# A gated attention and expert kernel: one stage order across the ends of token quarters, operand sums into buffers of their own, router inside the opening stage

## The reference, cut to what matters

```python
x = x + tanh(g_xattn[0]) * attention(layernorm(x), ctx_1024, Wq, Wk, Wv, Wo, bo)   # causal, 16 heads
x = x + tanh(g_ffn[0]) * ffn(layernorm(x))                                          # 4096 tokens x 512
...
scores = jax.nn.softmax(x @ router_w, axis=-1)             # 8 experts
topk_w, topk_idx = jax.lax.top_k(scores, 6)
g = jnp.einsum('td,edf->etf', x, w_gate)                   # 512 -> 256 each
u = jnp.einsum('td,edf->etf', x, w_up)
f_all = jnp.einsum('etf,efd->ted', jax.nn.silu(g) * u, w_down)
y = sum of the 6 picked f_all, each times its weight
y = y + _glu_mlp(hidden_states, ws_gate, ws_up, ws_down)   # shared, 512 -> 512
```

## Time and profile before

| | us |
|---|---|
| median of 3 runs | 1986.26 |
| lowest, highest | 1985.63, 1987.22 |
| profiled execution: span | 1984.3 |
| PE busy in it | 1888.9 |
| DVE busy | 1548.0 |
| ACT busy | 959.9 |
| POOL busy | 676.5 |

### The profile page before, as it was taken

The page is one execution under the profiler, slowest core; times in us unless marked ns, Lnnn a source line. Parts: engine busy times, 40 slices in busy tenths (PEclk is TensorE's granted clock), DMA queues, the critical chain, the costliest instruction groups (busy, mean ns, idle before and its releaser), DMA issues.

```text
span 1984.3 us, 33284 instructions
## 1 busy us (share of the span) xinstructions
PE 1888.9 (95%) x11664; PEld 1599.0 (81%) x11664; DVE 1548.0 (78%) x3333; ACT 959.9 (48%) x2252; POOL 676.5 (34%) x851
## 2 busy tenths in 40 slices
PE   6999999999998489999999999998999999899999
PEld 6899999999997368888867888876888887788887
DVE  5889888888888677787887777787777787777776
ACT  4777777777777343333433333343333343333332
POOL 3122132122221544343443334443334344433431
PEclk8999999999999689999999999999999999999999
DMA  7565565565554211212131121113121213111111
GB/s 208 131 146 129 142 148 127 139 147 132 140 123 145 85 43 54 75 54 64 61 119 44 54 82 64 58 43 108 63 85 49 68 54 114 56 54 53 51 46 43
DMA packets 148709, 178.60 MB, mean 90 GB/s; under 512 B 11200, under 2 KB 113600, under 8 KB 148544
## 3 DMA queue, kind: packets, MB, share of 16 engines
q1 hardware_dynamic: 148544, 176.48, 31.3%
HBM read 109.33 MB, written 16.78 MB: 64 GB/s over the span
## 4 chain that ended last, share of the span: by engine, by line
PE 50%; issue 5%; DVE 5%; POOL 4%; ACT 1%; DMA 0%; POOLq 0%; DVEq 0%; ACTq 0%
PE gate_up L1461 30%; PE down L1514 19%; POOL hidden L1096 2%; DVE ops_lo L939 2%; DVE acc L1306 1%; PE down L1443 1%; PE down L1429 1%; DVE h_lo L1295 1%; ACT ops_hi L932 1%; POOL w_sums L948 1%; POOL w_sums L953 0%; POOL w_sums L949 0%; POOL w_sums L951 0%; DVE gated L1273 0%; ACT h_hi L1154 0%
## 5 line engine op out<-in xcount | busy, mean ns | idle before, releaser
L1461 PE MATMUL gate_up<-xo_hi,ops_hi 128*128 128x512 f32 x1120 | 443.9, 396 | 25.7 <-DVE gated L1273 21.2
L1461 PE MATMUL gate_up<-xo_hi,ops_lo 128*128 128x512 f32 x1120 | 439.8, 393 | 0.0
L1461 PE MATMUL gate_up<-xo_lo,ops_hi 128*128 128x512 f32 x1120 | 439.4, 392 | 0.0
L1306 DVE SCALAR_TENSOR_TENSOR acc<-down,scale,acc 128x512 f32<-128x512 f32 x320 | 237.9, 748 | 55.0 <-PE down L1514 53.6
L1461 PEld LDWEIGHTS gate_up<-xo_hi,ops_hi 128*128 128x128 f32 x1120 | 212.4, 190 | 80.0 <-DVE gated L1273 26.7
L1514 PE MATMUL down<-d_hi,h_hi 128*128 128x512 f32 x640 | 249.9, 390 | 9.8 <-DVE acc L1306 5.1
L1514 PE MATMUL down<-d_lo,h_hi 128*128 128x512 f32 x640 | 249.1, 389 | 0.0
L1514 PE MATMUL down<-d_hi,h_lo 128*128 128x512 f32 x640 | 249.1, 389 | 0.0
L1461 PEld LDWEIGHTS gate_up<-xo_lo,ops_hi 128*128 128x128 f32 x1120 | 212.5, 190 | 45.1
L1461 PEld LDWEIGHTS gate_up<-xo_hi,ops_lo 128*128 128x128 f32 x1120 | 212.7, 190 | 43.3
L1096 POOL TENSOR_TENSOR hidden<-hidden,gated 128x512 f32<-128x512 f32 x120 | 158.9, 1330 | 206.7 <-DVE hidden L1278 170.7
(11 more groups left out here) (168 smaller groups left out, 4566.3 us busy)
## 6 DMA issues: line engine op xcount, KB each, us to landing
g_raw<-in_w_gate SPq DMA_DIRECT2D x40, 512.0 KB, 3.8
u_raw<-in_w_up SPq DMA_DIRECT2D x40, 512.0 KB, 3.8
d_raw<-in_w_down SPq DMA_DIRECT2D x40, 512.0 KB, 3.7
k_stack<-k_hi SPq DMA_DIRECT2D x128, 128.0 KB, 2.6
q_stack<-q_hi SPq DMA_DIRECT2D x128, 128.0 KB, 2.6
c_in<-in_ctx_t SPq DMA_DIRECT2D x16, 512.0 KB, 3.8
x_in<-in_x SPq DMA_DIRECT2D x16, 512.0 KB, 3.8
k_stack<-k_lo SPq DMA_DIRECT2D x64, 128.0 KB, 2.6
```

What stands on the lines that cost most here:

```text
L1306: dve.scalar_tensor_tensor(out=part, in0=ring("down", m, t)[:], scalar=scale[:, q, t, e:e + 1], in1=part, op0=ALU.mult, op1=ALU.add).then_ ...
L1461: ins = pe.matmul(gu_ps[bank][:], ops[x][:, which, a, c, :], xo[y][:, b, c, :], start=(begins and c == 0 and i == 0), stop=(c == CH - 1 an ...
```

## The change

1. One block instead of two. Each engine runs its attention stream and then its expert stream without a common end between them.
2. TensorE's order is that of a plain stage everywhere: gate, first half of the former down, up, second half. An opening stage does the downs of the closing stage before it. Only the last stage of all has its own downs behind it. The router's matmuls stand behind the gate of the opening stage, `back` behind the first half of the down.
3. `route` stands at the end of the opening stage on VectorE, behind the four adds; `shares` ahead of sum_22; `copy_logits` behind the low parts of the late weights.
4. `t_sum` becomes three buffers, so that T2 and T4 are no longer made in place, and the four sums stand in a row on GpSimd in the closing stage, ahead of the sums of up's weights. The low parts of T1 and T4 are made by GpSimd; VectorE keeps five. They have a semaphore of their own.
5. Rows of the next quarter are transposed at e = 6 and 8 (before 7 and 9), loads and statistics are one stage earlier too.
6. Stores of a finished quarter and loads of the new `acc` are issued in the opening stage. The scratch area at the start of SBUF is 1024 bytes, not 16384.

```diff
-        start, experts_block = experts(nc, ctx, x1, x1_stored, router, w_gate, w_up, w_down, out, ident, tanh_gates)
-        attention_block(start)
-        experts_block()
+        start, second = experts(nc, ctx, x1, x1_stored, router, w_gate, w_up, w_down, out, ident, tanh_gates)
+        first = attention_block(start)
+
+        with nc.Block() as block:
...
+            @block.tensor
+            def _(pe):
+                first.tensor(pe)
+                second.tensor(pe)
...
-    t_sum = sb("t_sum", [P, CH, BLK])
+    t_sum = [sb(f"t_sum{i}", [P, CH, BLK]) for i in range(3)]
...
-    ROWS_AT = (7, 9)
-    LOAD_AT, STATS_AT, NORM_AT = (4, 7), (5, 7), (6, 8)
+    ROWS_AT = (6, 8)
+    LOAD_AT, STATS_AT, NORM_AT = (3, 6), (4, 6), (5, 7)
...
+    XO = (B11, T2, B21, T1, T3, B22, T4)
+    ON_POOL = (T1, T4)
...
+            pool.tensor_tensor(t_sum[0][:], x_half(X12), x_half(X11), ALU.subtract).then_inc(x_sum_made, 1)
+            pool.wait_ge(x_sum_made, at + 1)
+            pool.tensor_tensor(t_sum[1][:], x_half(X22), t_sum[0][:], ALU.subtract).then_inc(x_sum_made, 1)
...
             if prepares:
                 x_first(n)
+                x_rest(n)
             if m + 1 < STAGES:
                 weights_sums(pool, 2 * m + 3)
-            if prepares:
-                x_second(n)
             for blk in GATED:
                 gate_hidden(m, blk)
             if prepares:
-                x_rest(n)
+                for b in ON_POOL:
+                    x_lo_by(pool, n, b)
...
             products(m, GATE)
             if opens(m):
-                back(q)
-            else:
+                for g in range(GROUPS):
+                    logits(q, g)
+            if m:
                 down(m - 1, 0)
+            if opens(m):
+                back(q)
             products(m, UP)
-            if not opens(m):
+            if m:
                 down(m - 1, 1)
-            if closes(m):
-                down(m, 0)
-                down(m, 1)
-                if n is not None:
-                    for g in range(GROUPS):
-                        logits(n, g)
+        down(STAGES - 1, 0)
+        down(STAGES - 1, 1)
```

More of the change, by code:

```diff
@@ L747, in attention @@
+        return Engines(sync, gpsimd, scalar, vector, tensor)
     return build
@@ L859, in ring_uses @@
     def ring_uses():
-        order = [("rows", 0, t) for t in range(TILES)] + [("logits", 0, g) for g in range(GROUPS)]
+        order = [("rows", 0, t) for t in range(TILES)]
         for m in range(STAGES):
@@ L867, in ring_uses @@
             if opens(m):
+                order += [("logits", q, g) for g in range(GROUPS)]
+            if m:
+                order += [("down", m - 1, t) for t in range(BT)]
+            if opens(m):
                 order.append(("back", q, 0))
-            else:
-                order += [("down", m - 1, t) for t in range(TILES)]
-            if closes(m):
-                order += [("down", m, t) for t in range(TILES)]
-                if n is not None:
-                    order += [("logits", n, g) for g in range(GROUPS)]
+            if m:
+                order += [("down", m - 1, t) for t in range(BT, TILES)]
+        order += [("down", STAGES - 1, t) for t in range(TILES)]
         return {use: k for k, use in enumerate(order)}
```

1732 lines of the change are left out of this document (868 added, 864 removed).

## The result

| | before | changed |
|---|---|---|
| median, us | 1986.74 (4 runs) | 1961.76 (4 runs) |
| lowest, highest | 1985.63, 1987.37 | 1959.79, 1963.31 |
| span of the profiled execution | 1984.3 | 1958.1 |

The ratio is 0.9877, with a 95% interval of 0.9865 to 0.9888: faster by 1.2%. The forecast was 1961.0 us, in a range of 1946 to 1974.

What follows compares the result with a forecast made beforehand. TensorE's own pace bounds plain stages; only waits at quarter ends and the opening were winnable. Three ends (22.8 us) plus opening (2.5) took 25.3 off the 1984.3 span: 1959.0, plus 1.96 for the median, 1961.0 us; range 1946 to 1974.

Steps and rivals of the forecast that it cites:

- The four terms of the walk: TensorE's predicted waits over one quarter end, stage by stage: sum 6.6 us, 7.1 with restarts, instead of 14.7.
- The turns: VectorE operations with both inputs in SBUF and GpSimd's run strictly one after the other; 2.3 us of GpSimd per 128x1024.
- rival "clock": Clock falls behind the gaps of 2.6 and 2.9 us: 2.5 us each end, 2.0 at the opening; 1970.5 us, chance 0.17.
- 2.9 us gap: At the opening, TensorE's wait for the third sum, ready at 731.1 but wanted at 728.2; 4.5 us before.
- No turns: GpSimd's work hides beside VectorE, 1.9 us left an end; 1945 us, chance 0.10.
- step 2: Tenth stage's downs move into the opening stage, half behind gate, half behind up; 4.1 us of waits gone.
- step 1: Route moves behind the adds on VectorE; the chain behind the 4.55 us wait for the third sum is gone.
- The barrier of 0.84 us: Wait of VectorE's first instruction in the second block, at 676.59; taken as the price of having two blocks.
- the 709 that was to show a misjudgement: First matmul of up in the opening, forecast at 711.2 us; standing before 709 would mean the opening was misjudged.
- Slower: Late low parts and route hold TensorE over 4.5 us in two stages, clock falls twice; 1993 us, chance 0.05.
- nothing: The change does nothing measurable because what stays sets the time; 1986 us, chance 0.03.
- Backlog doubled: VectorE's backlog is twice what was walked, each end keeps about 11 us; 1974 us, chance 0.10.

## Why the prediction was right, and where it was not

- **The sum.** 1961.0 forecast, 1961.76 measured. The change's share of the span is 23.6 us, 25.3 were forecast, so the term was 1.7 us too large; the difference of the medians lies between, well inside what executions of these kernels differ by.
- **A quarter.** 316.6 us were forecast, 317.23 measured, 324.28 before. What is left of each end is 7.6 us by the same count, 7.1 forecast, 14.7 before. The four terms of the walk, in order, forecast and measured over the matmuls' own time: closing stage up half 2.0 and 1.34; opening gate half 3.2 and 4.21; opening up half 0.5 and 0.88, of which 0.50 is the wait for sum_22 at 1031.31; next stage 0.9 and 0.88. The sum is good partly because two errors cancel.
- **Too large: the closing stage.** The turns were walked about right: d_lo took 1.55 us and two low parts of weights 2.23 and 2.22, 3.4 us over their times alone, as walked, and the second sum of up came 2.0 us late, 2.2 forecast. The third sum was waited for 1.05 us, 1.3 forecast. What was wrong is the 0.7 us for sum_22, which did not come. On VectorE it stands one h_lo behind the third sum:

```profile
988.79 0.68 DVE L1298 TENSOR_TENSOR hidden<-gate_up,second 128x512 f32<-128x512 f32 x1
989.39 0.68 DVE L1320 TENSOR_TENSOR h_lo<-hidden,h_hi 128x512 fp32r<-128x512 f32 x1
989.99 0.68 DVE L1303 TENSOR_TENSOR hidden<-gate_up,hidden 128x512 f32<-128x512 f32 x1
```

  It is done at 990.67, and behind P3's six matmuls, from 989.52 on, P4's first is due only at 991.02.
- **Wrong: the clock.** The forecast took it to hold behind a gap of 2.6 us. The gap came at 2.25 us, less than forecast, and the clock still fell at each of the three ends, at the first to 0.62 over 4.53 us, which cost 1.8 us; the wait for sum_22, forecast as 0.6, is hidden in it. The rival "clock" priced 2.5 us an end and some 9.5 in all; it came true in the opening stages at half that price, and did not in the first quarter of this execution, where no 2.9 us gap arose but one of 1.82; behind that the clock did fall in five of the experiments, so its holding here was partly luck. The claim "a granted clock of 1.00 through the end" was false.
- **Right: the turns.** T3's low part beside GpSimd's T4 was forecast near 2.9 us; the h_lo ahead of it took 2.90 and the pair T3, B22 3.90. "No turns" (1945) is refused by the rows of the changed kernel and by the run with all low parts on VectorE. The Trainium skill, "SBUF — State Buffer", section "Who interferes with whom", calls the shared ports an exclusive lock. The trace agrees: the h_lo took 2.90 us, and none of the 320 adds, which read PSUM, over 0.75. Moving the two low parts to GpSimd cost 6.6 us by these turns.
- **Incomplete: why the 4.55 us arose.** The prediction named route's place. Moved alone it gives 3 to 4.6 us, and a gap of 3.92 us remains. Moved back in the changed kernel it costs 5 us, nearly all in the first quarter, where no downs stand behind up, and 0.5 us at each later end. The cover by downs behind up is what closes the gap. The prediction credited step 2 only with the 4.1 us of waits in the downs; it owns most of step 1's gain too.
- **The opening.** The barrier of 0.84 us and the later copies measured as forecast (VectorE's copies 3.2 us earlier, 2.7 forecast). The first up half starts 0.7 us later than before against the x1 rows, 1.4 forecast, but in absolute time at 707.91, ahead of the 709 that was to show a misjudgement; 2.6 us of that come from attention. The gap of 2.9 us came as three waits, of 1.82, 0.57 and 0.23 us (one of 0.49 us for sum_22 stands in the up half before). The largest is for `first`, which the walk left out: ScalarE copies it behind the h_hi that waits for GpSimd's product. It hides most of VectorE's lateness, since the third sum came 2.4 us after TensorE would have wanted it, 2.9 forecast. From the first up half's start to the second stage's first down 4.1 us were saved, 4.4 forecast; from the x1 rows on 3.3, where the forecast had 3.0, and 2.5 with restarts.
- **The rivals.** "Slower" and "nothing" are refused by the result. "Backlog doubled" (1974) is refused by the 7.6 us at an end.

Open: what decides whether the clock falls behind a wait of 1.8 to 2.5 us (below), and what the separate buffers of the token sums and the earlier rows (parts 4 and 5 of the change) are worth by themselves, since no run has the new stage order without them.

## What to carry to other kernels

When the first busy engine waits at the turn of a loop, look first for independent work of its own that can stand in that place: 24 matmuls there closed a gap that moving the other engine's late work alone left at 3.9 us. On the engine that is waited for, put the results which release someone ahead of casts and adds that nobody wants yet, and price a move in the stage that receives it. Work between SBUF operands moved from VectorE to GpSimd beside VectorE's own was no relief here; taking it back was worth 6.6 us.

## What the runs showed of the hardware

- The granted clock behind an idle time of TensorE in the middle of full work is not decided by the length of the wait alone. Here are the waits from the first quarter's second stage on in the profiled executions of the fourteen kernels. The clock stayed at 1.00 behind every wait of 0.9 to 1.57 us. Behind 1.80 to 1.85 us it fell 6 times of 14, behind 2.23 to 2.26 us 10 of 12, behind 2.48 us 4 of 6, and behind 3.92 us and more all 10 times. It also stayed at 1.00 five times behind 2.76 to 3.03 us in the gate half of the first stage of all, with under 5 us of matmuls between that wait and the one before. The same kernel shows both: with route early the clock held behind this wait, and at the next end, behind 2.25 us, it fell, to 0.63 over 4.33 us:

```profile
1013.79 0.50 PE L1474 MATMUL gate_up<-xo_hi,ops_hi 128*128 128x512 f32 x1 [2.23 <-DVE gated L1298]
```

The stretch behind it (busy times, clock, DMA as above):

```profile
1013.79:1017.07 3.28, 3.09 (x12) 2.19 (x13) 3.28 (x6) 0.94 (x2) 0.00 (x0) 1.00 0.00 0
```

  With the token sums in two stages it fell behind 2.48 us (0.65), and in the run with shares and route at one place it held behind the same wait:

```profile
952.18:955.05 2.87, 2.87 (x13) 2.38 (x14) 1.38 (x2) 1.08 (x2) 0.00 (x0) 1.00 0.00 0
```

  Each fall cost 1.3 to 2.6 us over the next twelve matmuls (2.7 us at the full clock). So a wait of 1.8 us can already cost most of its own length again. What decides it stays open, so a difference of one or two us between two single executions can be this alone.
- The turns between VectorE and GpSimd hold for small tiles too: a 128x256 sum took 1.71 us in place of 0.73 beside low parts of 128x1024, and two h_lo of 0.6 us took 5.26. In these rows the short instruction pays the time of the long one that stands ahead of it.
